# Attention scores as plain fp32 on 64-row halves of the array, two heads side by side, in place of split fp32r over the whole array

## The chip, the core and the metric

The kernel runs on one core of one Trainium2 chip. The core has TensorE (PE; its weight loads are shown apart, as PEld), VectorE (DVE), ScalarE (ACT), GpSimd (POOL) and SyncE (SP), which issues most of the transfers. The metric is the device time of one execution in microseconds (us); less is better. Matmuls read SBUF and write PSUM, which has eight banks of 512 fp32 columns in each of 128 partitions.

## What is computed

Cross attention of 1024 queries over a context of 6404 keys, with 16 heads of 64, then the output projection, a residual and a layer norm:

```python
N_HEADS, D_MODEL, D_K, D_V = (16, 128, 64, 64)
Q = (input_Q @ W_Q).reshape(b, -1, N_HEADS, D_K).transpose(0, 2, 1, 3)
K = (input_K @ W_K).reshape(b, -1, N_HEADS, D_K).transpose(0, 2, 1, 3)
V = (input_V @ W_V).reshape(b, -1, N_HEADS, D_V).transpose(0, 2, 1, 3)
scores = jnp.einsum('bhqd,bhkd->bhqk', Q, K) / np.sqrt(D_K)
attn = jax.nn.softmax(scores, axis=-1)
context = jnp.einsum('bhqk,bhkd->bhqd', attn, V)
context = context.transpose(0, 2, 1, 3).reshape(b, -1, N_HEADS * D_V)
out = context @ W_O + input_Q
mu = jnp.mean(out, axis=-1, keepdims=True)
var = jnp.var(out, axis=-1, keepdims=True)
return (out - mu) / jnp.sqrt(var + 1e-05)
```

`input_Q` is x (1024 x 128), `input_K` and `input_V` are the context (6404 x 128). All of it is fp32.

## The kernel before

The heads go in 8 head pairs (128 columns of the weights each), the keys in 51 chunks of 128. Per head pair and chunk the kernel makes scores transposed, keys on the partitions and queries on the columns: for each head `s_ps[:, head, :]`, 128 keys by 1024 queries, two PSUM banks. ScalarE takes the exponential of each two banks into `probs` (L697, no maximum is subtracted), VectorE adds the probabilities up in `sums` (L828), and TensorE multiplies them with V into `o_ps` (`pv`, L453), head 0 on columns 0 to 63 of the array, head 1 on columns 64 to 127, so that both heads' results lie in the two halves of the partitions. At the end of a head pair a matmul with ones (L577) sums over partitions, VectorE inverts, GpSimd multiplies (L404).

Operands of the scores: K of a block of four chunks (512 keys) is projected into `kq_ps` (L419) for both heads at once; Q is projected for one head at a time with a weight tile `wq_dup` that holds the head's 64 columns twice (L425), so that Q stands in both partition halves. fp32r, the type of `k_parts` and `q_parts`, keeps fewer bits than fp32. ScalarE writes the high part of each (L681, L682 for K, L686 for Q), VectorE the rest, projection less high part (L797, L799, L805). `k_parts` holds for a head 64 rows of high parts of K and 64 rows of low parts, and `q_parts` holds Q's high part in both halves, then its low part in both halves. Each piece of the scores is thus two matmuls over all 128 rows: (K high, K low) with Q high, and with Q low, added in PSUM (L442). A chunk has 2 heads x 2 halves of the queries x 2 parts = 8 of them.

Every engine's program is written out by hand; each engine runs its own in order and waits on semaphores. On TensorE a step (L530) handles two chunks: scores of the one (L532), a projection of K or of the next pair's Q if one is due ("mid"), V of two chunks (L430), scores of the other chunk, the products with V of two earlier ones, and sometimes a Q projection at its "end". A head pair is one first step with a single chunk and 25 two-chunk steps, 18 of these in a hardware loop, 7 written out straight, in which the next pair's Q and K are projected. The scores of a head wait until the exponential of the chunk before has read its two banks (`probs_ready`, L438). `kq_ps` is one bank for all K and Q projections: each waits until the one before has been split (`kq_split`).

Of the kernel before, what the change touches and what calls it, by code (L numbers as in the profile page):

```python
# [4 lines left out]
F32 = mybir.dt.float32  # L5
F32R = mybir.dt.float32r
# [6 lines left out]
def cross_attention_kernel(nc: bass.Bass, xT: bass.AP, x: bass.AP, ctxT: bass.AP, w_q: bass.AP,  # L13
# [73 lines left out]
    PRO_USES = 5  # L87
# [3 lines left out]
    with ctx:  # L91
# [12 lines left out]
        wq_dup = sb("wq_dup", [P, 2, 2, 2, DH])  # L104
# [3 lines left out]
        k_parts = sb("k_parts", [P, 2, RING_COLS], F32R)  # L108
        q_parts = sb("q_parts", [P, 2, 2, 2, NQ], F32R)
# [34 lines left out]
        p_view = probs[:, 0:RING * 2 * NQ].rearrange("p (s h q) -> p s h q", s=RING, h=2)  # L144
# [7 lines left out]
        q0_ps = [o_ps[:, 0:QH], o_ps[:, QH:NQ], s_ps[:, 1, 0:QH], s_ps[:, 1, QH:NQ]]  # L152
# [13 lines left out]
        kq_high_ready = sem("kq_high_ready")  # L166
        kq_split = sem("kq_split")
# [242 lines left out]
        def _(pe):  # L410
            pe.sem_inc(pv_done, PV_CREDIT)

            def project_k(b_slot, parity, uses_before):

                n = TAIL_COLS if b_slot == TAIL_SLOT else BK
                if uses_before is not None:

                    pe.wait_ge(kq_split, uses_before)
# [14 lines left out]
            def scores(cols, parity, exps_before):  # L433

                for head in range(2):
                    if exps_before is not None:

                        pe.wait_ge(probs_ready, exps_before + head + 1)  # L438
                    for h in range(NQH):
                        q = slice(h * QH, (h + 1) * QH)  # L440
                        for part in range(2):
                            last = nc.tensor.matmul(s_ps[:, head, q], k_parts[:, head, cols:cols + P],  # L442
                                                    q_parts[:, parity, head, part, q],
                                                    start=(part == 0), stop=(part == 1))
                    last.then_inc(scores_ready, 1)

            def pv(p_slot, v_at, start, stop):

                for h in range(NQH):
                    q = slice(h * QH, (h + 1) * QH)  # L450
                    for head in range(2):
                        rows = slice(head * DH, (head + 1) * DH)
                        last = nc.tensor.matmul(o_ps[rows, q], v_ring[:, v_at[0], v_at[1], rows], p_view[:, p_slot, head, q],  # L453
                                                start=start, stop=stop)
# [14 lines left out]
            pe.wait_ge(wq0_loaded, 32)  # L469
            pe.wait_ge(x_loaded, 16)  # L470
            for n in range(4):
# [5 lines left out]
            pe.wait_ge(kq_split, PRO_USES)  # L477
            scores(0, 0, None)

            def pair_body(pair, parity, first, last):  # L480
# [5 lines left out]
                def chunk_scores(c, k, looped):  # L486

                    if k == CHUNKS and not looped:
                        if not last:

                            pe.wait_ge(kq_split, use(pair, PAIR_USES - 1))
                            scores(0, 1 - parity, 2 * (g0 + c - 1))
                        return
                    if k % BLOCK == 0:

                        if looped:
                            pe.wait_ge(kq_split, use(pair, 0) + (c - k) // BLOCK + k // BLOCK - 1)
                        else:
                            pe.wait_ge(kq_split, use(pair, k_use(k // BLOCK, last)))
                    scores(cols_of(k, looped), parity, 2 * (g0 + c - 1))  # L500

                def projection(c, k, looped, place):
# [5 lines left out]
                    if what == "q":  # L508
# [4 lines left out]
                        pe.wait_ge(kq_split, count - 1)  # L513
# [54 lines left out]
                for h in range(NQH):  # L568
                    if h == 0:

                        pe.wait_ge(kq_split, use(pair, LOOP_USES + len(straight_uses(last)) - 1))
# [3 lines left out]
                    for head in range(2):  # L575
                        rows = slice(head * DH, (head + 1) * DH)
                        last_mm = nc.tensor.matmul(den_ps[h][rows, :], ones[:, :],  # L577
                                                   sums[:, parity, head, h * QH:(h + 1) * QH], start=True, stop=True)
                    last_mm.then_inc(den_done, 1)

            def w_need(pair, parity, first):


                if first:
                    return 64
                return 32 * pair + (16 + 32 if parity else 64)
# [89 lines left out]
        def _(act):  # L676
            def high_k(slot):

                n = TAIL_COLS if slot == TAIL_SLOT else BK
                cols = slice(slot * BK, slot * BK + n)  # L680
                nc.scalar.activation(k_parts[0:DH, 0, cols], kq_ps[0:DH, 0:n], ACT.Copy)  # L681
                nc.scalar.activation(k_parts[DH:P, 1, cols], kq_ps[DH:P, 0:n], ACT.Copy).then_inc(kq_high_ready, 1)  # L682

            def high_q(src, n, parity):
                head, h = n // NQH, n % NQH
                nc.scalar.activation(q_parts[:, parity, head, 0, h * QH:(h + 1) * QH], src,  # L686
                                     ACT.Copy).then_inc(kq_high_ready, 1)

            def exps(g, p_slot):
# [5 lines left out]
                for head in range(2):  # L695
                    act.wait_ge(scores_ready, 2 * g + head + 1)
                    nc.scalar.activation(p_view[:, p_slot, head, :], s_ps[:, head, :], ACT.Exp,  # L697
                                         scale=SCALE).then_inc(probs_ready, 1)

            src_q = w_q[:, 0:2 * DH].rearrange("p (h n) -> p h n", h=2)  # L700
            for copy in range(2):
                act.dma_start(wq_dup[:, 0, :, copy, :], src_q).then_inc(wq0_loaded, 16)
            act.dma_start(xT_sb[:, :], xT).then_inc(x_loaded, 16)
            act.wait_ge(kq_proj_done, 1)
            high_k(0)
# [341 lines left out]
```

## Time and profile before

| | |
|---|---|
| median of 3 runs | 1790.04 us (1789.16 to 1790.11) |
| profiled execution, first to last instruction | 1789.5 us |
| TensorE busy | 1767.2 us, 99% |
| VectorE busy | 1266.8 us, 71% |
| ScalarE busy | 931.8 us, 52% |
| DMA, mean over the span | 18 GB/s |

The profiled execution is the 1789.5 us of the table; the runs are timed from outside. Busy time of an engine counts an instant once, even where records overlap: TensorE's matmul records overlap each other (a matmul's record begins when its columns start to flow and ends when the last result is out), so the starts of the records tell the pace and their lengths do not. A record of a weight load stands apart from its matmul. A plain fp32 matmul of the program has two load records and two matmul records, an fp32r one has one of each.

### The profile page before, as it was taken

To read this page: it belongs to the slowest core of one execution; us is meant where nothing else is said; L and a number is where in the kernel's file an instruction comes from. 1 tells how busy PE (TensorE), PEld (TensorE's weight loads), DVE (VectorE), ACT (ScalarE), POOL (GpSimd) and SP (SyncE) were. 2 spreads that over 40 slices of the span, in tenths; PEclk is the share of its full clock that TensorE was granted. 3 is DMA by queue.
4 is the path that set the end of the run, shared out by engine and by line. 5 is a ranking of instruction groups with operands and counts; after the bars stand their busy time and mean duration, and the time that the engine had idled before them with its cause. 6 is when DMAs were issued, how large, how long until landed. Compare 5 with 4: busy or idle time off the path is not lost.

```text
span 1789.5 us, 23718 instructions
## 1 busy us (share of the span) xinstructions
PE 1767.2 (99%) x7814; PEld 973.5 (54%) x7814; DVE 1266.8 (71%) x1376; ACT 931.8 (52%) x1079; POOL 21.3 (1%) x24
## 2 busy tenths in 40 slices
PE   9999999999999999999999999999999999999997
PEld 4555555555555555555555555555555555555555
DVE  5667667668667686667876677676786677776687
ACT  5555555555555555545555554555555555555552
POOL 0000000000000000000000000000000000000000
PEclk9999999999999999999999999999999999999999
DMA  2000000000000000000000000000000000000000
GB/s 80 12 18 18 13 21 18 12 18 12 22 18 18 12 22 15 17 18 12 22 18 12 18 18 17 18 18 12 18 22 12 18 18 12 16 18 12 18 1 13
DMA packets 25022, 31.41 MB, mean 18 GB/s; under 512 B 6384, under 2 KB 12528, under 8 KB 24944
## 3 DMA queue, kind: packets, MB, share of 16 engines
q1 hardware_dynamic: 24256, 29.78, 6.2%
q8 instruction: 41, 0.67, 0.2%
q10 hardware_dynamic: 688, 0.66, 0.1%
q14 instruction: 37, 0.30, 0.1%
HBM read 29.90 MB, written 0.52 MB: 17 GB/s over the span
## 4 chain that ended last, share of the span: by engine, by line
PE 98%; DVE 1%; issue 0%; DMA 0%; ACT 0%; POOLq 0%; POOL 0%; ACTq 0%
PE s_ps L442 44%; PE o_ps L453 41%; PE v_ps L430 5%; PE kq_ps L419 5%; PE kq_ps L425 1%; PE v_ps L577 0%; DMA xT_sb<-in_xT 0%; PE kq_ps L577 0%; DVE inv_sum L897 0%; PE o_ps L593 0%; DVE limits L841 0%; PE o_ps L425 0%; PE v_ps L593 0%; PE kq_ps L593 0%; PE s_ps L425 0%
## 5 line engine op out<-in xcount | busy, mean ns | idle before, releaser
L697 ACT ACTIVATE probs<-s_ps 128x1024 f32<-128x1024 f32 x816 | 793.0, 1024 | 777.8 <-PE s_ps L442 755.2
L828 DVE TENSOR_TENSOR sums<-sums,probs 128x1024 f32<-128x1024 f32 (+1 forms) x800 | 935.0, 1218 | 3.7 <-issue 0.5
L442 PE MATMUL s_ps<-q_parts,k_parts 128*128 128x512 f32 x3264 | 860.4, 405 | 7.5 <-DVE inv_sum L897 6.1
L453 PE MATMUL o_ps<-probs,v_ring 128*64 128x512 f32 x3264 | 746.3, 599 | 0.0
L442 PEld LDWEIGHTS s_ps<-q_parts,k_parts 128*128 128x128 f32 x3264 | 576.9, 188 | 285.8 <-issue 170.5
L453 PEld LDWEIGHTS o_ps<-probs,v_ring 128*64 128x64 f32 x3264 | 215.8, 136 | 419.0 <-issue 417.9
L815 DVE COPY v_ring<-v_ps 128x256 f32<-128x256 f32 (+1 forms) x209 | 87.4, 418 | 473.4 <-PE v_ps L430 473.4
L430 PEld LDWEIGHTS v_ps<-wv_sb,ctx_ring 128*128 128x128 f32 x816 | 123.4, 190 | 64.8 <-issue 56.1
L430 PE MATMUL v_ps<-wv_sb,ctx_ring 128*128 128x128 f32 x816 | 124.5, 274 | 0.0
L419 PE MATMUL kq_ps<-ctx_ring,wk_sb 128*128 128x512 f32 (+1 forms) x208 | 104.9, 586 | 0.0
L797 DVE TENSOR_TENSOR k_parts<-kq_ps,k_parts 64x512 fp32r<-64x512 f32 (+1 forms) x104 | 70.0, 673 | 9.7 <-ACT k_parts L682 6.5
L799 DVE TENSOR_TENSOR k_parts<-kq_ps,k_parts 64x512 fp32r<-64x512 f32 (+1 forms) x104 | 71.1, 683 | 1.4
L682 ACT ACTIVATE k_parts<-kq_ps 64x512 fp32r<-64x512 f32 (+1 forms) x104 | 60.9, 586 | 1.2
L681 ACT ACTIVATE k_parts<-kq_ps 64x512 fp32r<-64x512 f32 (+1 forms) x104 | 59.6, 573 | 3.2 <-PE kq_ps L419 3.2
L836 DVE RECIPROCAL inv_sum<-inv_sum 128x256 f32<-128x256 f32 x32 | 55.4, 1739 | 0.0
L419 PEld LDWEIGHTS kq_ps<-ctx_ring,wk_sb 128*128 128x128 f32 x208 | 39.3, 189 | 10.3 <-issue 1.6
L404 POOL TENSOR_TENSOR attn<-o_raw,inv_sum 128x512 f32 (+1 forms) x16 | 20.4, 1274 | 1749.3 <-DVE inv_sum L836 1749.3
L686 ACT ACTIVATE q_parts<-kq_ps 128x512 fp32r<-128x512 f32 x28 | 16.8, 600 | 25.2 <-PE kq_ps L425 25.2
L425 PE MATMUL kq_ps<-xT_sb,wq_dup 128*128 128x512 f32 x56 | 29.3, 604 | 0.0
L805 DVE TENSOR_TENSOR q_parts<-kq_ps,q_parts 128x512 fp32r<-128x512 f32 x28 | 19.2, 684 | 9.6 <-ACT q_parts L686 9.6
L740 ACT ACTIVATE o_raw<-o_ps 128x512 f32<-128x512 f32 x16 | 8.7, 594 | 21.1 <-PE o_ps L453 21.1
L841 DVE TENSOR_REDUCE limits<-inv_sum 128x1024 f32 (+1 forms) x16 | 19.2, 1206 | 0.0
(54 smaller groups left out, 112.5 us busy)
## 6 DMA issues: line engine op xcount, KB each, us to landing
ctx_ring<-in_ctxT SPq DMA_DIRECT2D x96, 256.0 KB, 2.6
ctx_ring<-in_ctxT SPq DMA_DIRECT2D x8, 130.0 KB, 2.4
wq_dup<-in_wq SPq DMA_DIRECT2D x14, 64.0 KB, 2.1
wk_sb<-in_wk SPq DMA_DIRECT2D x8, 64.0 KB, 2.3
wv_sb<-in_wv SPq DMA_DIRECT2D x8, 64.0 KB, 2.8
xT_sb<-in_xT ACTq DMA_DIRECT2D x1, 512.0 KB, 6.1
x_sb<-in_x SPq DMA_DIRECT2D x1, 512.0 KB, 5.4
wo_sb<-in_wo SPq DMA_DIRECT2D x1, 512.0 KB, 6.4
```

What stands on the lines that cost most here:

```text
L419: nc.tensor.matmul(kq_ps[:, 0:n], wk_sb[:, parity, :], ctx_ring[:, b_slot * BK:b_slot * BK + n], start=True, stop=True).then_inc(kq_proj_d ...
L430: return nc.tensor.matmul(v_ps[:, pos * P:(pos + 1) * P], ctx_ring[:, cols:cols + P], wv_sb[:, parity, :], start=True, stop=True)
L442: last = nc.tensor.matmul(s_ps[:, head, q], k_parts[:, head, cols:cols + P], q_parts[:, parity, head, part, q], start=(part == 0), stop=(p ...
L453: last = nc.tensor.matmul(o_ps[rows, q], v_ring[:, v_at[0], v_at[1], rows], p_view[:, p_slot, head, q], start=start, stop=stop)
L681: nc.scalar.activation(k_parts[0:DH, 0, cols], kq_ps[0:DH, 0:n], ACT.Copy)
L682: nc.scalar.activation(k_parts[DH:P, 1, cols], kq_ps[DH:P, 0:n], ACT.Copy).then_inc(kq_high_ready, 1)
L697: nc.scalar.activation(p_view[:, p_slot, head, :], s_ps[:, head, :], ACT.Exp, scale=SCALE).then_inc(probs_ready, 1)
L797: nc.vector.tensor_tensor(out=k_parts[DH:P, 0, cols], in0=kq_ps[0:DH, 0:n], in1=k_parts[0:DH, 0, cols].bitcast(F32), op=ALU.subtract)
L799: nc.vector.tensor_tensor(out=k_parts[0:DH, 1, cols], in0=kq_ps[DH:P, 0:n], in1=k_parts[DH:P, 1, cols].bitcast(F32), op=ALU.subtract).then ...
L815: nc.vector.tensor_copy(v_ring[:, group, pos:pos + n, :].rearrange("p n d -> p (n d)"), v_ps[:, pos * P:(pos + n) * P]).then_inc(v_ready, 1)
L828: nc.vector.tensor_tensor(out=sums[0:rows, parity, head, :], in0=sums[0:rows, parity, head, :], in1=p_view[0:rows, p_slot, head, :], op=AL ...
L836: nc.vector.reciprocal(inv_sum[:, n * w:(n + 1) * w], inv_sum[:, n * w:(n + 1) * w]).then_inc(inv_ready, 1)
```

## The change

`k_sb` and `q_sb` take the place of `k_parts` and `q_parts`: K and Q of a head pair in plain fp32, head 0 on partitions 0 to 63, head 1 on 64 to 127, as the projection leaves them. Nothing is split; VectorE's subtractions go, and ScalarE copies each projection in one instruction. Q is projected for both heads in one call, two calls per head pair in place of four, with `wq_sb` loaded once. The scores of a chunk are four matmuls: for each half of the queries, head 0 on rows 0 to 63 of the array and head 1 on rows 64 to 127. Both fill all 128 partitions of PSUM, in two banks. `s_ps` and `probs` are now ordered by half of the queries first and by head second; everything that reads them follows. `kq_taken`, counted by ScalarE, replaces `kq_high_ready` and `kq_split`.

```diff
@@ straight_uses
         if not last:
-            uses.update({(c, "mid"): ("q", 0), (c, "end"): ("q", 1), (c + 4, "mid"): ("q", 2),
-                         (c + 8, "mid"): ("q", 3), (c + 10, "mid"): ("k", 0)})
+            uses.update({(c, "mid"): ("q", 0), (c + 4, "mid"): ("q", 1), (c + 10, "mid"): ("k", 0)})
...
-    PRO_USES = 5
+    PRO_USES = 3
...
-        wq_dup = sb("wq_dup", [P, 2, 2, 2, DH])
+        wq_sb = sb("wq_sb", [P, 2, 2 * DH])
...
-        k_parts = sb("k_parts", [P, 2, RING_COLS], F32R)
-        q_parts = sb("q_parts", [P, 2, 2, 2, NQ], F32R)
+        k_sb = sb("k_sb", [P, RING_COLS])
+        q_sb = sb("q_sb", [P, 2, NQ])
...
-        q0_ps = [o_ps[:, 0:QH], o_ps[:, QH:NQ], s_ps[:, 1, 0:QH], s_ps[:, 1, QH:NQ]]
+        q0_ps = [o_ps[:, 0:QH], o_ps[:, QH:NQ]]
...
@@ sync: load_w
-                src_q = w_q[:, cols].rearrange("p (h n) -> p h n", h=2)
-                for copy in range(2):
-                    sp.dma_start(wq_dup[:, parity, :, copy, :], src_q).then_inc(w_loaded[parity], 16)
+                sp.dma_start(wq_sb[:, parity, :], w_q[:, cols]).then_inc(w_loaded[parity], 16)
...
@@ tensor
             def project_q(dst, n, parity):
 
-                head, h = n // NQH, n % NQH
-                nc.tensor.matmul(dst, wq_dup[:, parity, head, :, :].rearrange("p c n -> p (c n)"),
-                                 xT_sb[:, h * QH:(h + 1) * QH], start=True, stop=True).then_inc(kq_proj_done, 1)
+                nc.tensor.matmul(dst, wq_sb[:, parity, :], xT_sb[:, n * QH:(n + 1) * QH],
+                                 start=True, stop=True).then_inc(kq_proj_done, 1)
...
             def scores(cols, parity, exps_before):
 
-                for head in range(2):
+                for h in range(NQH):
                     if exps_before is not None:
 
-                        pe.wait_ge(probs_ready, exps_before + head + 1)
-                    for h in range(NQH):
-                        q = slice(h * QH, (h + 1) * QH)
-                        for part in range(2):
-                            last = nc.tensor.matmul(s_ps[:, head, q], k_parts[:, head, cols:cols + P],
-                                                    q_parts[:, parity, head, part, q],
-                                                    start=(part == 0), stop=(part == 1))
+                        pe.wait_ge(probs_ready, exps_before + h + 1)
+                    for head in range(2):
+                        rows = slice(head * DH, (head + 1) * DH)
+                        last = nc.tensor.matmul(s_ps[:, h, head * QH:(head + 1) * QH], k_sb[rows, cols:cols + P],
+                                                q_sb[rows, parity, h * QH:(h + 1) * QH], start=True, stop=True)
                     last.then_inc(scores_ready, 1)
...
@@ scalar
-            def high_k(slot):
+            def take_k(slot):
 
                 n = TAIL_COLS if slot == TAIL_SLOT else BK
-                cols = slice(slot * BK, slot * BK + n)
-                nc.scalar.activation(k_parts[0:DH, 0, cols], kq_ps[0:DH, 0:n], ACT.Copy)
-                nc.scalar.activation(k_parts[DH:P, 1, cols], kq_ps[DH:P, 0:n], ACT.Copy).then_inc(kq_high_ready, 1)
+                nc.scalar.activation(k_sb[:, slot * BK:slot * BK + n], kq_ps[:, 0:n], ACT.Copy).then_inc(kq_taken, 1)
...
-            def high_q(src, n, parity):
-                head, h = n // NQH, n % NQH
-                nc.scalar.activation(q_parts[:, parity, head, 0, h * QH:(h + 1) * QH], src,
-                                     ACT.Copy).then_inc(kq_high_ready, 1)
+            def take_q(src, n, parity):
+                nc.scalar.activation(q_sb[:, parity, n * QH:(n + 1) * QH], src, ACT.Copy).then_inc(kq_taken, 1)
...
@@ vector
-            def low_k(slot):
-
-                n = TAIL_COLS if slot == TAIL_SLOT else BK
-                cols = slice(slot * BK, slot * BK + n)
-                nc.vector.tensor_tensor(out=k_parts[DH:P, 0, cols], in0=kq_ps[0:DH, 0:n],
-                                        in1=k_parts[0:DH, 0, cols].bitcast(F32), op=ALU.subtract)
-                nc.vector.tensor_tensor(out=k_parts[0:DH, 1, cols], in0=kq_ps[DH:P, 0:n],
-                                        in1=k_parts[DH:P, 1, cols].bitcast(F32), op=ALU.subtract).then_inc(kq_split, 1)
```

The first place is on TensorE, a two-chunk step of the loop with a K projection: `s_ps` are the scores, `kq_ps` the projection of K, `v_ps` that of V, `o_ps` the product with V; x4 counts calls, and the ISA and REGISTER_ALU rows set registers for the waits. Before:

```order
L442 MATMUL s_ps<-q_parts,k_parts 128x512 x4
L438 REGISTER_ALU
L442 MATMUL s_ps<-q_parts,k_parts 128x512 x4
L519 ISA
L419 MATMUL kq_ps<-ctx_ring,wk_sb 128x512
L536 ISA
L430 MATMUL v_ps<-wv_sb,ctx_ring 128x128 x2
L438 ISA
L442 MATMUL s_ps<-q_parts,k_parts 128x512 x4
L438 REGISTER_ALU
L442 MATMUL s_ps<-q_parts,k_parts 128x512 x4
L453 MATMUL o_ps<-probs,v_ring 64x512 x4
```

The same place of the changed kernel:

```order
L435 MATMUL s_ps<-q_sb,k_sb 128x512 x2
L432 REGISTER_ALU
L435 MATMUL s_ps<-q_sb,k_sb 128x512 x2
L511 ISA
L414 MATMUL kq_ps<-ctx_ring,wk_sb 128x512
L528 ISA
L424 MATMUL v_ps<-wv_sb,ctx_ring 128x128 x2
L432 ISA
L435 MATMUL s_ps<-q_sb,k_sb 128x512 x2
L432 REGISTER_ALU
L435 MATMUL s_ps<-q_sb,k_sb 128x512 x2
L445 MATMUL o_ps<-probs,v_ring 64x512 x4
```

Nothing has moved; each four calls of the scores over 128 rows are two calls over 64 rows.

The second place is on TensorE too, the first straight steps of a head pair, where the next pair's Q is projected into `kq_ps` from `xT_sb`. Before:

```order
L442 MATMUL s_ps<-q_parts,k_parts 128x512 x8
L425 MATMUL kq_ps<-xT_sb,wq_dup 128x512
L430 MATMUL v_ps<-wv_sb,ctx_ring 128x128 x2
L442 MATMUL s_ps<-q_parts,k_parts 128x512 x8
L453 MATMUL o_ps<-probs,v_ring 64x512 x8
L425 MATMUL kq_ps<-xT_sb,wq_dup 128x512
L442 MATMUL s_ps<-q_parts,k_parts 128x512 x8
L419 MATMUL kq_ps<-ctx_ring,wk_sb 128x512
```

The same place of the changed kernel:

```order
L435 MATMUL s_ps<-q_sb,k_sb 128x512 x4
L419 MATMUL kq_ps<-xT_sb,wq_sb 128x512
L424 MATMUL v_ps<-wv_sb,ctx_ring 128x128 x2
L435 MATMUL s_ps<-q_sb,k_sb 128x512 x4
L445 MATMUL o_ps<-probs,v_ring 64x512 x8
L435 MATMUL s_ps<-q_sb,k_sb 128x512 x4
L414 MATMUL kq_ps<-ctx_ring,wk_sb 128x512
```

The Q projection that stood between a product with V and the scores is gone; of the two later ones, both beside V projections, the first stays and the second is gone.

## Rows read from the trace of the kernel before

**Rows 1.** The page: busy us (share) xinstructions, and the chain by line.

```profile
PE 1767.2 (99%) x7814; PEld 973.5 (54%) x7814; DVE 1266.8 (71%) x1376; ACT 931.8 (52%) x1079; POOL 21.3 (1%) x24
...
PE s_ps L442 44%; PE o_ps L453 41%; PE v_ps L430 5%; PE kq_ps L419 5%; PE kq_ps L425 1%; PE v_ps L577 0%; DMA xT_sb<-in_xT 0%; PE kq_ps L577 0%; DVE inv_sum L897 0%; PE o_ps L593 0%; DVE limits L841 0%; PE o_ps L425 0%; PE v_ps L593 0%; PE kq_ps L593 0%; PE s_ps L425 0%
```

**Rows 2.** Spans and granted clock.

```profile
core 0: 1789.5 us, clock 0.998
```

**Rows 3.** Groups: line engine op, shapes xcount | busy us, mean ns | idle before, releaser.

```profile
L442 PE MATMUL s_ps<-q_parts,k_parts 128*128 128x512 f32 x3264 | 860.4, 405 | 7.5 <-DVE inv_sum L897 6.1
L453 PE MATMUL o_ps<-probs,v_ring 128*64 128x512 f32 x3264 | 746.3, 599 | 0.0
...
L430 PE MATMUL v_ps<-wv_sb,ctx_ring 128*128 128x128 f32 x816 | 124.5, 274 | 0.0
...
L797 DVE TENSOR_TENSOR k_parts<-kq_ps,k_parts 64x512 fp32r<-64x512 f32 (+1 forms) x104 | 70.0, 673 | 9.7 <-ACT k_parts L682 6.5
```

**Rows 4.** Timeline of TensorE's matmuls: start us, length us, line, shapes xrecords.

```profile
208.61 1.02 PE L425 MATMUL kq_ps<-xT_sb,wq_dup 128*128 128x512 f32 x2
209.47 0.61 PE L430 MATMUL v_ps<-wv_sb,ctx_ring 128*128 128x128 f32 x4
...
211.85 3.65 PE L453 MATMUL o_ps<-probs,v_ring 128*64 128x512 f32 x16
215.43 2.11 PE L442 MATMUL s_ps<-q_parts,k_parts 128*128 128x512 f32 x8
217.38 1.02 PE L419 MATMUL kq_ps<-ctx_ring,wk_sb 128*128 128x512 f32 x2
218.24 0.61 PE L430 MATMUL v_ps<-wv_sb,ctx_ring 128*128 128x128 f32 x4
...
220.62 3.65 PE L453 MATMUL o_ps<-probs,v_ring 128*64 128x512 f32 x16
...
927.49 3.65 PE L453 MATMUL o_ps<-probs,v_ring 128*64 128x512 f32 x16
...
935.44 1.08 PE L453 MATMUL o_ps<-probs,v_ring 128*64 128x512 f32 x4
```

**Rows 5.** Timeline of TensorE's weight loads in a product with V.

```profile
220.61 0.20 PEld L453 LDWEIGHTS o_ps<-probs,v_ring 128*64 128x64 f32 x4 [0.35 <-issue]
...
214.05 0.14 PEld L453 LDWEIGHTS o_ps<-probs,v_ring 128*64 128x64 f32 x2 [0.29 <-issue]
214.48 0.14 PEld L453 LDWEIGHTS o_ps<-probs,v_ring 128*64 128x64 f32 x2 [0.29 <-issue]
```

**Rows 6.** Timeline of matmuls around the changes of shape, cut to single ones.

```profile
214.90 0.60 PE L453 MATMUL o_ps<-probs,v_ring 128*64 128x512 f32 x2
215.43 0.50 PE L442 MATMUL s_ps<-q_parts,k_parts 128*128 128x512 f32 x1
...
220.07 0.61 PE L442 MATMUL s_ps<-q_parts,k_parts 128*128 128x512 f32 x2
220.62 0.65 PE L453 MATMUL o_ps<-probs,v_ring 128*64 128x512 f32 x2
```

**Rows 7.** The scores line: xrecords: least/median/most ns of one.

```profile
L442 PE MATMUL s_ps<-q_parts,k_parts x3264: 387/393/796, 13.1 to 1756.9; 128*128 128x512 f32 x192
```

**Rows 8.** Timeline of the start.

```profile
0.74 1.00 ACTq L702 DMA_DIRECT2D wq_dup<-in_wq  x2
...
10.03 0.60 ACT L686 ACTIVATE q_parts<-o_ps 128x512 fp32r<-128x512 f32 x1 [0.26 <-PE o_ps L425]
...
12.38 0.69 DVE L805 TENSOR_TENSOR q_parts<-s_ps,q_parts 128x512 fp32r<-128x512 f32 x1 [0.17 <-ACT q_parts L686]
...
13.12 2.11 PE L442 MATMUL s_ps<-q_parts,k_parts 128*128 128x512 f32 x8 [1.19 <-DVE q_parts L805]
```

**Rows 9.** Timeline of ScalarE in one step.

```profile
216.75 1.94 ACT L697 ACTIVATE probs<-s_ps 128x1024 f32<-128x1024 f32 x2 [3.68 <-PE s_ps L442]
...
219.17 0.59 ACT L682 ACTIVATE k_parts<-kq_ps 64x512 fp32r<-64x512 f32 x1
```

More of the change, by code:

```diff
@@ L5 @@
 F32 = mybir.dt.float32
-F32R = mybir.dt.float32r
 I32 = mybir.dt.int32
@@ L452, in pv @@
                         rows = slice(head * DH, (head + 1) * DH)
-                        last = nc.tensor.matmul(o_ps[rows, q], v_ring[:, v_at[0], v_at[1], rows], p_view[:, p_slot, head, q],
-                                                start=start, stop=stop)
+                        last = nc.tensor.matmul(o_ps[rows, q], v_ring[:, v_at[0], v_at[1], rows],
+                                                p_view[:, p_slot, h, head * QH:(head + 1) * QH], start=start, stop=stop)
                 last.then_inc(pv_done, 1)
@@ L467, in _ @@
             project_k(0, 0, None)
-            pe.wait_ge(wq0_loaded, 32)
+            pe.wait_ge(wq0_loaded, 16)
             pe.wait_ge(x_loaded, 16)
-            for n in range(4):
+            for n in range(NQH):
                 project_q(q0_ps[n], n, 0)
@@ L569, in pair_body @@
                     if h == 0:
-                        pe.wait_ge(kq_split, use(pair, LOOP_USES + len(straight_uses(last)) - 1))
+                        pe.wait_ge(kq_taken, use(pair, LOOP_USES + len(straight_uses(last)) - 1))
                     else:
@@ L577, in pair_body @@
                         last_mm = nc.tensor.matmul(den_ps[h][rows, :], ones[:, :],
-                                                   sums[:, parity, head, h * QH:(h + 1) * QH], start=True, stop=True)
+                                                   sums[:, parity, h, head * QH:(head + 1) * QH], start=True, stop=True)
                     last_mm.then_inc(den_done, 1)
@@ L584, in w_need @@
                 if first:
-                    return 64
-                return 32 * pair + (16 + 32 if parity else 64)
+                    return 48
+                return 24 * pair + (16 + 24 if parity else 48)
             run_pairs(pe, pair_body)
@@ L818, in add_sums @@
             def add_sums(g, p_slot, parity, new, rows):
-                for head in range(2):
-                    dve.wait_ge(probs_ready, 2 * g + head + 1)
+                for h in range(NQH):
+                    dve.wait_ge(probs_ready, NQH * g + h + 1)
                     if new:
-                        nc.vector.tensor_copy(sums[:, parity, head, :], p_view[:, p_slot, head, :]).then_inc(sums_done, 1)
+                        nc.vector.tensor_copy(sums[:, parity, h, :], p_view[:, p_slot, h, :]).then_inc(sums_done, 1)
                     else:
-                        dve.wait_ge(sums_done, 2 * g + head + (SUM_CREDIT - 1))
-                        nc.vector.tensor_tensor(out=sums[0:rows, parity, head, :], in0=sums[0:rows, parity, head, :],
-                                                in1=p_view[0:rows, p_slot, head, :], op=ALU.add).then_inc(sums_done, 1)
+                        dve.wait_ge(sums_done, NQH * g + h + (SUM_CREDIT - 1))
+                        nc.vector.tensor_tensor(out=sums[0:rows, parity, h, :], in0=sums[0:rows, parity, h, :],
+                                                in1=p_view[0:rows, p_slot, h, :], op=ALU.add).then_inc(sums_done, 1)
             def invert_sums(pair, n):
@@ L853, in pair_body @@
                 g0 = CHUNKS * pair
-                def low_halves(c, k, looped, place):
-                    found = use_in(pair, c, k, looped, place, last)
-                    if found is not None:
-                        count, what, b, s = found
-                        dve.wait_ge(kq_high_ready, count)
-                        if what == "q":
-                            low_q(kq_ps[:, :], b, 1 - parity)
-                        else:
-                            low_k(s)
                 def step(c, k, looped):
```

57 lines of the change are left out of this document (20 added, 37 removed).

## The prediction

> **What bounds the kernel now.** I read the busy shares first: TensorE is busy 99% of the span, and of the chain of work that ended last 44% stands in the scores line, 41% in the line of probabilities times V and 11% in the projections [rows 1]. The granted clock is 0.998 of full speed, the 2.4 GHz level [rows 2]. So what counts is how much time TensorE's own stream takes; a microsecond saved on ScalarE or VectorE is worth nothing as long as nobody waits for them. TensorE's waits for others are 7.5 us before the scores in all, 6.1 of them for the copies of the sums at the ends of head pairs [rows 3].
>
> Then the stream itself, in order of time [rows 4]. A two-chunk step (the step from 211.85 to 220.62 takes 8.77 us, with a K projection; the one from 927.49 to 935.44 takes 7.95, without) is: product with V of two chunks, scores of one chunk, projections, scores of the next chunk, again the product. Three paces are to be seen:
> - The product with V is plain fp32 in two 64-column halves of the array, with the records of the two heads side by side: their weight loads start in twos, 0.43 us apart [rows 5]. A plain fp32 matmul has two records (1632 calls, 3264 records [rows 3]). One chunk is 4 calls, 8 records, 4 such twins: 1.72 us, and 16 records would be 3.44 of the 3.58 that they take.
> - The scores are one-record fp32r matmuls over the whole array, 8 per chunk. From 215.43 to the K projection at 217.38 are 1.95 us, of which 0.11 is the late first load (below), so 1.84. From the V projection at 218.24 to the product at 220.62 are 2.38; less 4 x 0.11 for V (three steps make the 0.61 long group out of records of 0.27) and 0.10 before the product, 1.84 to 1.85 stay for the scores.
> - A change of the array's shape costs. The last twins of the product start at 214.90 and would be fed by 215.33, the first scores matmul starts at 215.43: 0.10 us. Its record is 0.50 long where the line's median is 0.39: 0.11 more, since its load starts with it and not before [rows 6, 7]. Towards the product the same is 0.09 (220.07 plus two steps of 0.23 is 220.53, start 220.62) and 0.05 for a 64-column load (0.65 against 0.60) [rows 6]. Between scores and projections, all 128x128, nothing of the kind stands: the K projection's two records take 0.86 and V follows [rows 4].
>
> **The change part by part.** *Scores.* 8 records of 128x128 become 4 calls on 64x128 halves, 8 records of plain fp32. No row of this trace shows row halves at work. The nearest is the product with V, which splits the array the other way, has the same 512 columns and the same two records per call. If the two halves overlap as those do, a chunk is 4 x 0.43 = 1.72 us where it is 1.85: 0.13 less, times 408 chunks = **-53 us**. The other end is no overlap: 8 x 0.43 = 3.44, +1.59 a chunk, +649 us. A gain over the first end would need a twin under 0.43 us, and every two-record fp32 matmul of 512 columns in the trace, whole array or half, keeps that pace (the K projection too, 0.86 for its two records [rows 4]). I take the first, because the twin rows are the same kind of work.
>
> By the Trainium skill ("TensorE: Matmul & The Clock Gate", Measured speedup vs the span model) four row tiles ran 3.07 times as fast as one after the other. Two row tiles would by that overlap too, and the -53 stand; a page's figure, which no run here shows yet.
>
> *Switches.* Before, a two-chunk step has two changes of shape: scores to product, product to scores. Now the scores are 64x128, the projections stay 128x128, the product 128x64. The order on TensorE is unchanged (first place above), so each step now has four: product to scores, scores to projection, projection to scores, scores to product. The two new ones both lead to a load of 128 columns: 0.10 + 0.10 = 0.20 each, as product to scores. A head pair has 25 two-chunk steps and one first step with a single new switch: 8 x (25 x 2 + 1) = 408 switches, **+82 us**. Bounds: 0 (+0 us), if full array and row halves need no emptying between them; 0.10 (+41), if only the emptying is paid; 0.14 (+57), the price towards the product; 0.21 (+86). I take 0.20 because each new switch ends in the same load of 128 columns as the row at 215.43.
>
> The Trainium skill ("TensorEngine Tiling (Array Packing)", Key Properties) says that a change of the tiling mode drains TensorE and a change of the tile alone does not, and lists 64x128 as a mode of its own. The rows here show it for 128x128 against 128x64 alone. By that rule the +82 are due; without it for row halves the sum would be 68 us below today instead of 14 above, which is the first rival.
>
> *Q projection.* Four calls of 0.86 us (208.61 to 209.47) per head pair become two [rows 4]: 7 x 2 x 0.86 = **-12 us**, wholly on the chain, as TensorE is never idle there. The one that followed the product is gone with them (second place above), and the two that stay stand beside V projections, where they add no switch of their own.
>
> *Start.* Before the first scores stand two more Q projections and all low parts, and the scores start at 13.12. After, the second Q copy on ScalarE (0.60 from 10.03) is the last thing needed: 10.63, and 0.05 more (the last low part is over at 13.07, the scores start at 13.12), so 10.7, 2.4 earlier; xT is issued one weight transfer of 0.50 us sooner, at most 0.5 more [rows 8]. **-3 us**.
>
> *K and Q copies.* On VectorE 104 + 104 subtractions of K and 32 of Q go (70.0 us in the one line, as much in the other, and 32 x 0.69 = 22), on ScalarE two 64-row copies become one of 128 rows (2 x 0.59 to about the 0.60 of the Q copy) [rows 3, 8, 9]. Both engines are off the chain (71% and 52% busy), so **0**. The SP queue issues one weight transfer less per head pair, also 0.
>
> *Does a wait come up?* The scores of a half of a chunk wait for the exponential of the same bank pair of the chunk before; behind that wait stands all of TensorE's queue. After the change: first half of the scores fed 0.10 + 0.86 after their start, records end 0.17 later, exponential from about 1.17, the second one 0.92 to 0.97 behind it (two take 1.94 [rows 9]) and over by 3.1. TensorE wants them at 1.92 + 0.10 + 0.10 + 0.44 + 0.10 = 2.6 for the first half (exponential over at 2.2) and 3.5 for the second: 0.4 us of cover each. 0, and each 0.1 missing would cost 20 us over 200 steps.
>
> Sum against the profiled span of 1789.5: -53 + 82 - 12 - 3 = +14, 1803.5; 0.5 us lie around it (median 1790.0), so **1804**.
>
> **Rivals.**
> *A: row halves switch cheaply.* The step keeps two dear switches; the other 408 cost nothing: -53 - 12 - 3 = -68, **1722**. With 0.10 each it is -27, 1763; with 0.14, -11, 1779; at 0.16 to 0.17 the change is nil. So it decides from 0.17 downwards. For it: no row shows this switch, and half the array's rows could be loaded while the other half still runs. Against it: in the trace each change of shape, in both directions, has its gap.
> *B: the halves do not overlap fully.* Two scores matmuls write two banks with all 128 partitions at once, where the two of the product share one bank's partitions. If these outputs go one after the other: +649 instead of -53, about **2506**; if each twin is only a tenth slower, +70, 1874. It decides as soon as a twin takes more than 0.43. The trace has no row for it or against it.
> *C: the records of a call stay in order*, head 0 twice, then head 1 twice, so that each run of scores begins and ends with half the array idle: +0.43 per chunk, +175, **1979**. Against it: the product is written in the same order and its first two loads (0.20 us for four of them at 220.61) already start together [rows 5].
> *D: the change is not what it says*: ScalarE's exponentials come too late and TensorE waits, for instance 0.2 us in each of 200 steps, +40, 1844. Against it the 0.4 us of cover.
>
> **How the numbers follow.** Forecast (switches at 0.17 to 0.22, full overlap): 0.60. A: 0.28, of which 1722 about 0.08, the part between 0.10 and 0.16 about 0.20 with 0.08 of it within 3.6 us of 1790. B 0.06, C 0.03, D 0.03. A difference of 0.2% (3.6 us) is about what a measurement of this kernel can tell from none. Of the forecast's own spread a small part, 0.04, also falls within it. So faster 0.20, same 0.12, slower 0.68. The range leaves about 0.08 below (free switches) and 0.09 above (B, C): 1755 to 1840.
>
> **What would show it.** In the timeline of TensorE: scores in 8 records whose starts come in twos 0.43 us apart, one chunk 1.72 (else B or C: starts 0.43 apart singly); between scores and projection, and back, a gap of about 0.10 and a first record 0.10 too long (else A); no idle time of TensorE put down to the probabilities (else D); a step without a K projection at 7.95 + 2 x 0.20 - 2 x 0.13 = 8.09 us; first scores at 10.2 to 10.7. VectorE's share falls to about 61%, ScalarE's to about 48%. The prediction is wrong if the step is below 7.95.

## The result, and the profile after

The changed kernel takes 1803.41 us (1803.13 to 1804.75, 3 runs) against 1790.04: the ratio is 1.0076, with a 95% interval of 1.0062 to 1.0089. Run again beside another kernel it took 1803.01, ratio 1.0072 (1.0056 to 1.0087). It is slower by three quarters of a percent; forecast was 1804.

The page after. Its first rows answer to [rows 1] and give busy time of each engine and the chain by line:

```profile
PE 1780.2 (99%) x7782; PEld 668.2 (37%) x7782; DVE 1096.6 (61%) x1136; ACT 868.9 (48%) x959; POOL 21.3 (1%) x24
...
PE s_ps L435 43%; PE o_ps L445 41%; PE v_ps L424 6%; PE kq_ps L414 6%; PE kq_ps L419 1%; PE v_ps L569 0%; PE kq_ps L569 0%; DVE inv_sum L848 0%; DMA ctx_ring<-in_ctxT 0%; PE o_ps L585 0%; DVE limits L811 0%; PE v_ps L585 0%; PE kq_ps L585 0%; PE o_ps L419 0%; POOLq L89 0%
```

VectorE lost 170 us of work and ScalarE 63, and nothing came of it: TensorE is still the bound at 99%. The share of the chain in the scores fell from 44% to 43%, that of the projections rose from 11% to 13%.

The groups, as in [rows 3]: the scores and the two projections whose cost changed without a change of their own.

```profile
L435 PE MATMUL s_ps<-q_sb,k_sb 64*128 64x512 f32 x3264 | 810.9, 615 | 6.9 <-DVE inv_sum L848 6.1
L445 PE MATMUL o_ps<-probs,v_ring 128*64 128x512 f32 x3264 | 746.2, 599 | 0.0
...
L424 PE MATMUL v_ps<-wv_sb,ctx_ring 128*128 128x128 f32 x816 | 134.2, 286 | 0.0
L414 PE MATMUL kq_ps<-ctx_ring,wk_sb 128*128 128x512 f32 (+1 forms) x208 | 115.3, 636 | 0.9 <-DMA ctx_ring<-in_ctxT 0.9
```

The scores' busy time fell by 49.5 us (860.4 to 810.9). V's rose by 9.7 (124.5 to 134.2) and K's by 10.4 (104.9 on the page before): the late first loads. The emptying itself lies between records or under their tails and is not in any busy time; it has to be read from starts. The ends of TensorE's records are modelled in the profile, so a length is used here only against another of the same kind, and each price is read from starts too.

The timeline of TensorE's matmuls, a step without and one with a K projection, to be set beside [rows 4]:

```profile
914.63 3.65 PE L445 MATMUL o_ps<-probs,v_ring 128*64 128x512 f32 x16
918.21 1.99 PE L435 MATMUL s_ps<-q_sb,k_sb 64*128 64x512 f32 x8
920.13 0.71 PE L424 MATMUL v_ps<-wv_sb,ctx_ring 128*128 128x128 f32 x4
920.77 1.99 PE L435 MATMUL s_ps<-q_sb,k_sb 64*128 64x512 f32 x8
922.69 3.65 PE L445 MATMUL o_ps<-probs,v_ring 128*64 128x512 f32 x16
926.27 1.99 PE L435 MATMUL s_ps<-q_sb,k_sb 64*128 64x512 f32 x8
928.19 1.13 PE L414 MATMUL kq_ps<-ctx_ring,wk_sb 128*128 128x512 f32 x2
929.15 0.61 PE L424 MATMUL v_ps<-wv_sb,ctx_ring 128*128 128x128 f32 x4
929.69 1.99 PE L435 MATMUL s_ps<-q_sb,k_sb 64*128 64x512 f32 x8
931.61 0.65 PE L445 MATMUL o_ps<-probs,v_ring 128*64 128x512 f32 x2
```

A step without a K projection takes 922.69 - 914.63 = 8.06 us (7.95 in the step shown before), one with a K projection 931.61 - 922.69 = 8.92 (8.77). The scores of a chunk, start to next start, are 1.92, the product 3.58 as before.

The same timeline cut to single records around the changes of shape, as [rows 6], and the weight loads of one chunk's scores:

```profile
919.60 0.59 PE L435 MATMUL s_ps<-q_sb,k_sb 64*128 64x512 f32 x2
920.13 0.38 PE L424 MATMUL v_ps<-wv_sb,ctx_ring 128*128 128x128 f32 x1
...
920.77 0.70 PE L435 MATMUL s_ps<-q_sb,k_sb 64*128 64x512 f32 x2
...
928.19 0.70 PE L414 MATMUL kq_ps<-ctx_ring,wk_sb 128*128 128x512 f32 x1
```

```profile
918.21 0.30 PEld L435 LDWEIGHTS s_ps<-q_sb,k_sb 64*128 64x128 f32 x4 [0.81 <-issue]
918.75 0.19 PEld L435 LDWEIGHTS s_ps<-q_sb,k_sb 64*128 64x128 f32 x2 [0.24 <-issue]
919.17 0.19 PEld L435 LDWEIGHTS s_ps<-q_sb,k_sb 64*128 64x128 f32 x2 [0.23 <-issue]
```

The scores' records stand in twos. The last two start at 919.60, would be fed by 920.03, and V starts at 920.13: 0.10 of emptying. V's first record is 0.38 long where 0.27 is usual, K's 0.70 where 0.59 is, the scores' first 0.70 against 0.59: 0.11 for a late load each time. The starts say the same: from V to the scores behind it are 920.77 - 920.13 = 0.64, which is 4 x 0.11 for V, 0.10 for the late load and 0.10 of emptying. The loads of the scores, in twos after the first four, are 0.42 to 0.43 apart: both row halves of the array work at the same time, each twin at the 0.43 of the product's.

### The profile page after: what moved, and what is told of

Same layout as the page of the kernel before. It is cut to its first block, busy times and chain, and to the rows that moved or that the text cites. A ratio compares the mean times of both kernels' runs of the same rounds, so it can differ in the third digit from the quotient of the medians.

```text
span 1801.5 us, 23142 instructions
## 1 busy us (share of the span) xinstructions
PE 1780.2 (99%) x7782; PEld 668.2 (37%) x7782; DVE 1096.6 (61%) x1136; ACT 868.9 (48%) x959; POOL 21.3 (1%) x24
## 4 chain that ended last, share of the span: by engine, by line
PE 98%; DVE 1%; issue 0%; DMA 0%; ACT 0%; POOLq 0%; POOL 0%; SPq 0%; ACTq 0%
PE s_ps L435 43%; PE o_ps L445 41%; PE v_ps L424 6%; PE kq_ps L414 6%; PE kq_ps L419 1%; PE v_ps L569 0%; PE kq_ps L569 0%; DVE inv_sum L848 0%; DMA ctx_ring<-in_ctxT 0%; PE o_ps L585 0%; DVE limits L811 0%; PE v_ps L585 0%; PE kq_ps L585 0%; PE o_ps L419 0%; POOLq L89 0%
## 5 line engine op out<-in xcount | busy, mean ns | idle before, releaser
L798 DVE TENSOR_TENSOR sums<-sums,probs 128x1024 f32<-128x1024 f32 (+1 forms) x800 | 924.8, 1217 | 0.8 <-issue 0.8
L435 PE MATMUL s_ps<-q_sb,k_sb 64*128 64x512 f32 x3264 | 810.9, 615 | 6.9 <-DVE inv_sum L848 6.1
L435 PEld LDWEIGHTS s_ps<-q_sb,k_sb 64*128 64x128 f32 x3264 | 280.5, 185 | 393.0 <-issue 336.3
L424 PE MATMUL v_ps<-wv_sb,ctx_ring 128*128 128x128 f32 x816 | 134.2, 286 | 0.0
L414 PE MATMUL kq_ps<-ctx_ring,wk_sb 128*128 128x512 f32 (+1 forms) x208 | 115.3, 636 | 0.9 <-DMA ctx_ring<-in_ctxT 0.9
L672 ACT ACTIVATE k_sb<-kq_ps 128x512 f32<-128x512 f32 (+1 forms) x104 | 61.3, 590 | 4.2 <-PE kq_ps L414 4.2
L414 PEld LDWEIGHTS kq_ps<-ctx_ring,wk_sb 128*128 128x128 f32 x208 | 30.9, 188 | 80.5 <-issue 80.5
L419 PE MATMUL kq_ps<-xT_sb,wq_sb 128*128 128x512 f32 x28 | 15.8, 645 | 0.0
L794 DVE COPY sums<-probs 128x1024 f32<-128x1024 f32 x16 | 10.3, 677 | 2.7 <-ACT probs L685 2.7
L675 ACT ACTIVATE q_sb<-kq_ps 128x512 f32<-128x512 f32 x14 | 8.4, 598 | 0.0
```

The costliest lines, as they stand in the source:

```text
L414: nc.tensor.matmul(kq_ps[:, 0:n], wk_sb[:, parity, :], ctx_ring[:, b_slot * BK:b_slot * BK + n], start=True, stop=True).then_inc(kq_proj_d ...
L419: nc.tensor.matmul(dst, wq_sb[:, parity, :], xT_sb[:, n * QH:(n + 1) * QH], start=True, stop=True).then_inc(kq_proj_done, 1)
L424: return nc.tensor.matmul(v_ps[:, pos * P:(pos + 1) * P], ctx_ring[:, cols:cols + P], wv_sb[:, parity, :], start=True, stop=True)
L435: last = nc.tensor.matmul(s_ps[:, h, head * QH:(head + 1) * QH], k_sb[rows, cols:cols + P], q_sb[rows, parity, h * QH:(h + 1) * QH], start ...
L672: nc.scalar.activation(k_sb[:, slot * BK:slot * BK + n], kq_ps[:, 0:n], ACT.Copy).then_inc(kq_taken, 1)
L798: nc.vector.tensor_tensor(out=sums[0:rows, parity, h, :], in0=sums[0:rows, parity, h, :], in1=p_view[0:rows, p_slot, h, :], op=ALU.add).th ...
```

## The experiments

**The price of a change of shape, without row halves.** The kernel before; only V is projected otherwise:

```diff
-                return nc.tensor.matmul(v_ps[:, pos * P:(pos + 1) * P], ctx_ring[:, cols:cols + P],
-                                        wv_sb[:, parity, :], start=True, stop=True)
+                for half in range(2):
+                    keys = slice(half * DH, (half + 1) * DH)
+                    last = nc.tensor.matmul(v_ps[keys, pos * P:(pos + 1) * P],
+                                            ctx_ring[:, cols + half * DH:cols + (half + 1) * DH],
+                                            wv_sb[:, parity, :], start=True, stop=True)
+                return last
```

> The kernel before, with V alone projected in two calls of 64 columns of the array (keys 0 to 63 and 64 to 127 of a chunk) in place of one of 128. The work of V stays 0.44 us per two chunks, since its two halves overlap; the scores stay fp32r over the whole array, so no row half is in it. Theory (any change of the array's shape costs 0.10 us of emptying and a late load, 0.05 for 64 columns, 0.10 for 128): two new changes in each of 200 two-chunk steps, scores or K to V at 0.15 and V to scores at 0.20: +70 us, 1860. Rival (the gaps around the projections of the changed kernel belong to row halves, not to changes of shape): no new cost, 1790.

Measured: 1856.24 us (1856.15 to 1856.45), ratio to the kernel before 1.0366 (1.0349 to 1.0383), +65.8 us against the 1790.49 beside it. The rival is gone: the same arithmetic, split over two column halves, costs 66 us because the shape changes twice more per step. Timeline of TensorE in one of its steps:

```profile
929.59 2.11 PE L446 MATMUL s_ps<-q_parts,k_parts 128*128 128x512 f32 x8
931.63 0.66 PE L432 MATMUL v_ps<-wv_sb,ctx_ring 128*64 128x128 f32 x8
932.21 2.14 PE L446 MATMUL s_ps<-q_parts,k_parts 128*128 128x512 f32 x8
934.28 0.65 PE L457 MATMUL o_ps<-probs,v_ring 128*64 128x512 f32 x2
```

The scores ahead of V now take 2.04 us to the next start (1.95 in [rows 4]), V 0.58, the scores behind it 2.07. From the first scores to the next product it is 934.28 - 929.59 = 4.69; in the kernel before it is 4.37, the 7.95 of [rows 4] less 3.58 for the product. That is 0.32 a step, where the theory had 0.35. No change of shape is cheaper for that: the 0.03 lie in the kernel before. Its steps without a K or Q projection take 935.44 - 933.02 = 2.42 from V to the next product, where the step with K takes 2.38 [rows 4]. Timeline of the kernel before, V and then the weight loads of the scores behind it:

```profile
933.02 0.60 PE L430 MATMUL v_ps<-wv_sb,ctx_ring 128*128 128x128 f32 x4
...
933.38 0.76 PEld L442 LDWEIGHTS s_ps<-q_parts,k_parts 128*128 128x128 f32 x4
934.30 0.78 PEld L442 LDWEIGHTS s_ps<-q_parts,k_parts 128*128 128x128 f32 x4 [0.15 <-ACT probs L697]
```

The loads there stand behind waits for the exponentials and come a little late: 81 such waits of loads in the kernel before, 16 in this run, whose V takes longer. Over the whole of both traces, the median step without a projection goes from 7.95 to 8.26 us (+0.31), with a K or Q projection from 8.76 or 8.77 to 9.12 (+0.35, the theory's figure).

**The load that follows is part of the price.** The changed kernel with the edit above for V, and K and Q in the same manner:

```diff
-                nc.tensor.matmul(kq_ps[:, 0:n], wk_sb[:, parity, :], ctx_ring[:, b_slot * BK:b_slot * BK + n],
-                                 start=True, stop=True).then_inc(kq_proj_done, 1)
+                for head in range(2):
+                    rows = slice(head * DH, (head + 1) * DH)
+                    last = nc.tensor.matmul(kq_ps[rows, 0:n], wk_sb[:, parity, rows],
+                                            ctx_ring[:, b_slot * BK:b_slot * BK + n], start=True, stop=True)
+                last.then_inc(kq_proj_done, 1)
```

> The changed kernel, with all projections of K, Q and V in calls of 64 columns of the array in place of 128. The number of changes of shape per two-chunk step stays four, but the one from the scores to a projection now waits for a 64-column load (0.05) and not for a 128-column one (0.10), and the first step of a head pair loses the change from V to the product. Theory (price is emptying plus the load that follows): 200 x 0.05 + 8 x 0.05 + 8 x 0.15, about -11 us, 1792. Rival (a change has one price, whatever is loaded after it): only the 8 changes of the first steps go, -1.6 us, 1802.

Measured: 1790.40 us, ratio to the kernel before 1.0002 (0.9992 to 1.0012), 13.0 us under the changed kernel's 1803.41. The theory's sum was 11.6; the rest, 1.4 us between medians of two sets of runs, is not accounted for. The timeline shows the two new prices in a step without a K projection:

```profile
928.68 1.99 PE L445 MATMUL s_ps<-q_sb,k_sb 64*128 64x512 f32 x8
930.60 0.66 PE L432 MATMUL v_ps<-wv_sb,ctx_ring 128*64 128x128 f32 x8
931.18 1.99 PE L445 MATMUL s_ps<-q_sb,k_sb 64*128 64x512 f32 x8
933.10 3.65 PE L455 MATMUL o_ps<-probs,v_ring 128*64 128x512 f32 x16
```

V takes 0.58 to the next start in place of 0.64, the two scores 1.92 as before, and from the first scores to the product it is 4.42 in place of 4.48. A change of shape is thus not one price: it is 0.10 of emptying and whatever load has to come behind it. With this alone the changed kernel is level with the one before.

**What a Q projection costs.** The changed kernel with each Q projection issued twice:

```diff
             def project_q(dst, n, parity):
 
+                nc.tensor.matmul(dst, wq_sb[:, parity, :], xT_sb[:, n * QH:(n + 1) * QH], start=True, stop=True)
                 nc.tensor.matmul(dst, wq_sb[:, parity, :], xT_sb[:, n * QH:(n + 1) * QH],
                                  start=True, stop=True).then_inc(kq_proj_done, 1)
```

> The changed kernel, with each projection of Q issued twice, so that a head pair has four calls again as before. Theory (TensorE's stream is the bound and a 512-column projection costs its two records of 0.43 us): 16 x 0.86 = +13.8 us, 1817. Rival (the calls are hidden in waits at the places where they stand): under +3 us, 1806 or less.

Measured: 1817.90 us (1816.88 to 1819.45), +14.5 on 1803.4. The 14 extra calls within head pairs cost what was reckoned: the median step with a Q projection goes from 8.92 to 9.78 us, 0.86 more. Two more calls stand before the first scores, and there this run's profile is slow, for a cause that stays open. From its timeline:

```profile
7.78 1.91 PE L419 MATMUL o_ps<-xT_sb,wq_sb 128*128 128x512 f32 x2
...
9.48 1.66 PE L420 MATMUL o_ps<-xT_sb,wq_sb 128*128 128x512 f32 x2
```

The first of these calls takes 9.48 - 7.78 = 1.70 us, twice the usual 0.86. So the surplus over 13.8 lies within what the start varies by. A call of Q is on the chain at its full 0.86 us, and so the removed ones saved as much.

**The cover of the exponentials.** The changed kernel with the projections behind both chunks' scores:

```diff
                     chunk_scores(*todo[0], looped)
+                    if len(todo) > 1:
+                        chunk_scores(*todo[1], looped)
 
                     projection(c, k, looped, "mid")
...
                     group.then_inc(v_proj_done, 1)
-                    if len(todo) > 1:
-                        chunk_scores(*todo[1], looped)
...
-                        if n == 0:
-                            take_projection(c, k, looped, "mid")
-                    take_projection(c, k, looped, "end")
+                    take_projection(c, k, looped, "mid")
```

> The changed kernel, with the projections behind the scores of both chunks of a step (scores, scores, K or Q, V, product), ScalarE's copies of them behind both exponentials. One change of shape less per step (three: 0.20 + 0.20 + 0.15, against four), -0.20 x 200 = -40 us, but nothing stands between the two scores. Theory (the exponential of the same banks is over 2.2 us after the first scores began, and they are wanted at 1.8 and some 0.1 for the wait): +0.5 us of waiting a step, +100, net +60 us, 1863. Rival (the cover is larger than worked out, TensorE never waits for ScalarE): net -40 us, 1763, which would be a better order.

Measured: 1885.26 us (1885.11 to 1886.60), ratio to the kernel before 1.0530 (1.0513 to 1.0548), +81.9 on the changed kernel. The direction is the theory's, the wait larger than it said. Timeline of TensorE's matmuls, then one row of its weight loads and the waits of the whole run (engine, tile and line <- releaser: us, times, longest):

```profile
925.72 1.99 PE L435 MATMUL s_ps<-q_sb,k_sb 64*128 64x512 f32 x8
927.97 2.04 PE L435 MATMUL s_ps<-q_sb,k_sb 64*128 64x512 f32 x8 [0.27 <-ACT probs L685]
929.95 0.71 PE L424 MATMUL v_ps<-wv_sb,ctx_ring 128*128 128x128 f32 x4
```

```profile
927.97 0.19 PEld L435 LDWEIGHTS s_ps<-q_sb,k_sb 64*128 64x128 f32 x2 [1.09 <-ACT probs L685]
...
PEld s_ps L435 <- ACT probs L685: 341.3, 399, 1.2
...
PE s_ps L435 <- ACT probs L685: 54.4, 200, 0.4
```

The second scores are wanted at 925.72 + 1.82 = 927.54 and start at 927.97, 2.25 us after the first. That is 0.43 of waiting, 0.10 for the load that waits with them (it could not be fetched ahead, since the wait stands before the load), and 0.06 more at their second half: 4.23 from start to V in place of 3.64, 0.59. Less the change of shape saved (0.20), 0.39 x 200 = 78 us; the scores' waits for the copies of the sums at the ends of head pairs add 3.3 us (9.4 in all, 6.1 in the changed kernel). So the V projection between the two scores is not only work, it is the cover under which ScalarE empties the banks.

**A step with two changes of shape.** From these: keep something between the two scores, but of their shape, and give the rest the product's shape. V of two chunks goes on row halves (a single V, as in the first step of a head pair, on column halves), each half into a bank of its own, since the two row halves must not write one bank at once (the Trainium skill, "TensorEngine Tiling (Array Packing)", Gotcha 1; not tried here). VectorE adds the halves. K and Q go behind the product on column halves.

```diff
+            def project_v_rows(cols0, parity0, cols1, parity1):
+
+                for n, (cols, par) in enumerate(((cols0, parity0), (cols1, parity1))):
+                    for half, dst in enumerate((v_ps, kq_ps)):
+                        rows = slice(half * DH, (half + 1) * DH)
+                        last = nc.tensor.matmul(dst[:, n * P:(n + 1) * P], ctx_ring[rows, cols:cols + P],
+                                                wv_sb[rows, par, :], start=True, stop=True)
+                return last
...
-                    projection(c, k, looped, "mid")
-
                     pe.wait_ge(v_ready, groups(pair, -1) + (c + 1) // 2)
...
+                        pe.wait_ge(kq_taken, taken_by(pair, c, k, looped, last))
...
-                    projection(c, k, looped, "end")
+                    projection(c, k, looped, "mid")
...
+                    nc.vector.tensor_copy(v_part[:, :], kq_ps[:, 0:2 * P]).then_inc(v_part_ready, 1)
+                    dve.wait_ge(v_part_ready, part)
+                    nc.vector.tensor_tensor(out=v_ring[:, group, :, :].rearrange("p n d -> p (n d)"), in0=v_ps[:, 0:2 * P],
+                                            in1=v_part[:, :], op=ALU.add).then_inc(v_ready, 1)
```

> The changed kernel without the two new changes of shape. V of the two chunks is projected on row halves too, the first 64 model dimensions on rows 0 to 63 into v_ps and the last 64 on rows 64 to 127 into kq_ps, and VectorE adds the two on the way to v_ring (one more instruction of 256 columns and one wait of its own per step). K and Q are projected in 64-column calls at the end of a step, behind the product, which has that shape. A two-chunk step is then scores, V, scores on row halves and product, K or Q on column halves: two changes of shape instead of four. Theory (the 408 new changes cost what the changed kernel lost, and the second scores are wanted 0.44 us of V after the first, just when their exponential is over): step without K 7.67 us and up to 0.1 of waiting, against 8.06, so -0.3 to -0.39 x 200 and -2 for the first steps: 1723 to 1743. Rival (the time is in the row halves themselves, not in the changes): 1790 to 1803. Second rival (ScalarE becomes the limit between the two scores, 0.4 us a step as in the order with late projections): 1803.

Measured: 1752.66 us (1752.06 to 1753.38, 5 runs), ratio to the kernel before 0.9792 (0.9778 to 0.9805); 50.4 us under the changed kernel run beside it. It is the fastest of all kernels here, and still 10 us above the range that the theory gave. Timeline of TensorE (the scores and the product; V stands between in eight single records), then one of ScalarE, then the weight loads of the second scores:

```profile
912.96 3.65 PE L472 MATMUL o_ps<-probs,v_ring 128*64 128x512 f32 x16
916.54 1.99 PE L462 MATMUL s_ps<-q_sb,k_sb 64*128 64x512 f32 x8
...
918.81 2.03 PE L462 MATMUL s_ps<-q_sb,k_sb 64*128 64x512 f32 x8
920.77 3.65 PE L472 MATMUL o_ps<-probs,v_ring 128*64 128x512 f32 x16
924.25 1.03 PE L424 MATMUL kq_ps<-ctx_ring,wk_sb 128*64 128x512 f32 x4
```

```profile
917.72 1.94 ACT L713 ACTIVATE probs<-s_ps 128x1024 f32<-128x1024 f32 x2 [3.62 <-PE s_ps L462]
919.97 1.94 ACT L713 ACTIVATE probs<-s_ps 128x1024 f32<-128x1024 f32 x2 [0.31 <-PE s_ps L462]
```

```profile
918.79 0.30 PEld L462 LDWEIGHTS s_ps<-q_sb,k_sb 64*128 64x128 f32 x4
919.71 0.30 PEld L462 LDWEIGHTS s_ps<-q_sb,k_sb 64*128 64x128 f32 x4 [0.61 <-ACT probs L713]
```

A step is 920.77 - 912.96 = 7.81 us against 8.06. The first scores and V run through without a gap (916.54 to 918.81 is 0.10 + 1.72 + 0.45). The second scores take 1.96 to the product where 1.82 would do: 0.14 too long. The exponentials begin at 917.72, 1.18 after the scores, as reckoned in the prediction, and the first is over in time: the scores start at 918.81, when they are wanted. But the wait stands before the weight load, so the load comes at 918.79 and not under V's matmuls: about 0.10. The load of the second half, at 919.71 behind the second exponential, is about 0.05 late in the same way. The theory allowed 0.1 in all. So 7.67 + 0.14 = 7.81, and 200 x 0.25 = 50 us. The second rival, a limit by ScalarE, gets 0.14 a step, 28 us; the first none. The two changes of shape gave back 0.39 (0.25 and 0.14) where the prediction had charged 0.40.

**The changed kernel again**, beside the one above:

> The changed kernel itself, beside the other kernel of this call on the same chip: 1803, and nothing to tell apart.

Measured: 1803.01 us (1802.45 to 1803.49).

## Why the prediction was right, point by point

- *Scores, -53.* The twins keep 0.43 us, as the column halves do; no overlap is lost. The scores are 1.72 now, the 1.92 from start to start less emptying and first load. Before they were 1.84 to 1.85 in the steps that the prediction read. In the steps without a projection those behind V took some 0.03 more (2.42 against 2.38, above), and there the gain is larger than 0.13.
- *Switches, +82.* 0.10 of emptying and 0.10 to 0.11 of late load at each new change, as read from the product's rows, now also between row halves and the whole array. The Trainium skill's rule ("TensorEngine Tiling (Array Packing)", Key Properties), that a change of mode drains TensorE, agrees with the trace for 64x128 too. The figure of 0.10 is the trace's, and it is only half of the 82: the prediction said that by that rule the +82 were due, but the rule speaks of the emptying (+41), and the late load (+41) rests on the rows alone.
- *The two together.* A step came out at 8.06 for the 8.09 forecast and at 8.92 with a K projection. Over all steps of both traces the medians rose by 0.11 without a projection and by 0.15 with one of K or Q. That is about +27 us of the run, where the two terms gave +29. Most of the difference is what the scores behind V had lost before.
- *Q, -12.* Added up over the steps it is 12 us, and the doubled projections cost 0.86 each as reckoned.
- *Start, -3.* The timeline of the start shows the first scores, with the wait that ends before them:

```profile
6.05 1.10 PE L414 MATMUL kq_ps<-ctx_ring,wk_sb 128*128 128x512 f32 x2 [0.88 <-DMA ctx_ring<-in_ctxT]
...
6.99 1.88 PE L419 MATMUL o_ps<-xT_sb,wq_sb 128*128 128x512 f32 x4
...
8.90 0.60 ACT L675 ACTIVATE q_sb<-o_ps 128x512 f32<-128x512 f32 x1 [0.26 <-PE o_ps L419]
...
9.55 0.70 PE L435 MATMUL s_ps<-q_sb,k_sb 64*128 64x512 f32 x2 [0.47 <-ACT q_sb L675]
```

  9.55 against 13.12 in [rows 8] is 3.6 us, not 3, and lies outside the 10.2 to 10.7 that was to be seen. The last Q copy starts at 8.90 and not at 10.03. But the profiled execution before had a late start of its own, a wait for xT. The kernel before with V in halves has the same instructions up to there, and in its trace nothing waits for xT. First the row of the kernel before, then two of that run:

```profile
8.04 1.96 PE L425 MATMUL o_ps<-xT_sb,wq_dup 128*128 128x512 f32 x4 [1.33 <-DMA xT_sb<-in_xT]
```

```profile
6.50 1.96 PE L425 MATMUL o_ps<-xT_sb,wq_dup 128*128 128x512 f32 x4
...
11.63 2.11 PE L446 MATMUL s_ps<-q_parts,k_parts 128*128 128x512 f32 x8 [1.08 <-DVE q_parts L809]
```

  Against 11.63 the gain is 2.1 us, by one profile each. In the changed kernel the Q projections come right behind that of K, which waits for the context (6.05, 6.99), so an earlier xT brings nothing more. So the 3.6 is in part luck, and against a start without that wait the term was 0.9 too large.
- *No new wait, 0.* The waits before the scores are 6.9 us on the page (7.5 before). The prediction's 2.6 us until the first half is wanted has 0.10 too much in its sum, which gives 2.66; the rows give 920.77 - 918.21 = 2.56. ScalarE's timeline has the exponentials in between:

```profile
919.39 1.94 ACT L685 ACTIVATE probs<-s_ps 128x1024 f32<-128x1024 f32 x2 [3.56 <-PE s_ps L435]
```

  The first is over 1.02 later, at 920.4, so the cover is nearly 0.4. Some weight loads do wait for the exponentials (92 times, 29.9 us), but are there before the scores need them. The late-projection order, which takes away 0.44 of V and two changes of shape from between the scores, waits.
- *Around the span, and the luck in it.* The profiled spans went from 1789.5 to 1801.5, +12.0: about +27 for the steps, -12 for Q and -3.6 for the start. The forecast of +14 was 2 us too high for this. The prediction took 0.5 us to lie around the span, from a median and another run's span; in runs that list both it is about 1.8 (1803.23 and 1801.4). That is 1.3 too little, and it offsets most of the 2. By the same 1.8 the profiled execution before was one of 1791.3 us, 1.3 above the median, which is about what its late start cost; so the medians moved by 13.4 where the spans moved by 12.0. The mechanism was right and each large term within 2 us; that the median came out within 1 us of the forecast is partly luck.

Rival A (cheap switches) falls with the rows at 919.60 and with both projection experiments, B and C with the twins, D with the waits.

## What to carry to other kernels

Where TensorE is the bound, count the changes of the array's shape in the inner loop as instructions: here each cost 0.10 us of emptying and a load of 0.05 (64 columns) to 0.11 us (128 columns) that nothing hid, and 408 more of them took the whole gain of the faster scores, the fewer projections and the earlier start, and 13 us on top. The split of the scores paid here (1752.66 us) only when what stood between them had the same split. V could be cut into halves of either direction at the same pace (0.44 to 0.45 us for two chunks), so its shape could follow its neighbours. And before moving work from between two steps, see whose latency it covers.

## What had not been expected

- The projection of V in column halves, the same arithmetic, cost 66 us between scores over the whole array; between scores on row halves, with K and Q cut too, it saved 13. The split of the neighbours decides, not the work.
- A wait in front of a matmul also holds back its weight load, so that a wait which ends just in time still costs the load: 0.10 of the 0.59 us with late projections, and about 0.10 of the 0.14 in the fastest kernel.
- Row halves write twice 128 partitions at once, into two banks, at the pace of column halves that write 128 together: 0.43 us per twin in both.
